# Packing the first query block's maxima scores into the PSUM banks of the third: ten pieces per group in place of eleven

## What is computed

```python
scores = jnp.einsum('bhsd,bhtd->bhst', xq, keys) * scale
scores = jnp.where(causal, scores, -jnp.inf)
probs = jax.nn.softmax(scores, axis=-1)
out = jnp.einsum('bhst,bhtd->bhsd', probs, values)
```

## Time and profile before

| what | value |
|---|---|
| median of 3 runs | 722.67 us |
| lowest and highest | 719.99 and 726.54 us |
| the profiled execution's own time | 722.22 us |
| its span, first to last instruction | 720.5 us (1.7 us lie outside it) |
| PE busy | 687.2 us, 95% of the span |
| DVE, ACT, POOL busy | 413.9, 293.0, 237.1 us |
| attention stage | about 70 to 345 us of the span |

### The profile page before, as it was taken

The page is one execution under the profiler, slowest core; times in us unless marked ns, Lnnn a source line. Parts: engine busy times, 40 slices in busy tenths (PEclk is TensorE's granted clock), DMA queues, the critical chain, the costliest instruction groups (busy, mean ns, idle before and its releaser), DMA issues. The chain is left out here.

```text
span 720.5 us, 10111 instructions
## 1 busy us (share of the span) xinstructions
PE 687.2 (95%) x3606; PEld 518.6 (72%) x3606; DVE 413.9 (57%) x982; ACT 293.0 (41%) x548; POOL 237.1 (33%) x241
## 2 busy tenths in 40 slices
PE   8998999999999999999999999789999999978998
PEld 6876666666666666666787788567888888766886
DVE  6735966766767676663477630485455544634611
ACT  4213345555545555454345132363434344322321
POOL 4465022322322232222245344232234222203443
PEclk9999999999999999999999999879999999997999
DMA  9328615123213333111356300210001100103211
GB/s 293 111 89 236 130 45 148 46 73 73 73 42 92 86 82 73 49 41 46 105 154 200 136 1 1 56 53 29 30 30 48 41 30 1 41 2 101 60 58 59
DMA packets 23146, 55.19 MB, mean 77 GB/s; under 512 B 3732, under 2 KB 4088, under 8 KB 22040
## 3 DMA queue, kind: packets, MB, share of 16 engines
q1 hardware_dynamic: 22840, 54.41, 26.5%
q10 hardware_dynamic: 256, 0.13, 0.1%
HBM read 42.86 MB, written 11.54 MB: 75 GB/s over the span
## 5 line engine op out<-in xcount | busy, mean ns | idle before, releaser
L964 DVE CUSTOM_DVE_ANT_0 bank<-bank,mask 128x512 f32<-128x512 f32 (+3 forms) x256 | 118.3, 521 | 60.8 <-PE bank L1018 60.5
L219 POOL TENSOR_TENSOR up_w_lo<-up_w_eff,up_w_hi 128x512 fp32r<-128x512 f32 x50 | 66.3, 1335 | 121.2 <-ACT up_w_hi L215 121.2
L372 POOL TENSOR_TENSOR down_h_lo<-hidden,down_h_hi 128x512 fp32r<-128x512 f32 x50 | 65.8, 1316 | 106.7 <-ACT down_h_hi L367 106.6
L52 PE MATMUL bank<-x0T_hi,up_w_hi 128*128 128x512 f32 x224 | 96.5, 431 | 3.8 <-POOL up_w_lo L219 2.3
L918 ACT ACTIVATE probs<-bank 128x512 f32<-128x512 f32 x160 | 85.1, 597 | 28.1 <-PE bank L1040 25.4
L54 PE MATMUL bank<-x0T_lo,up_w_hi 128*128 128x512 f32 x224 | 89.0, 398 | 0.0
L53 PE MATMUL bank<-x0T_hi,up_w_lo 128*128 128x512 f32 x224 | 89.0, 397 | 0.0
L52 PE MATMUL bank<-down_w_hi,down_h_hi 128*128 128x512 f32 x200 | 79.4, 397 | 1.1 <-DVE down_w_lo L357 0.7
L883 POOL TENSOR_SCALAR_AFFINE_SELECT probs<-probs 128x512 f32<-128x512 f32 x64 | 40.0, 638 | 120.8 <-ACT probs L918 120.8
L53 PE MATMUL bank<-down_w_hi,down_h_lo 128*128 128x512 f32 x200 | 78.9, 395 | 0.0
L54 PE MATMUL bank<-down_w_lo,down_h_hi 128*128 128x512 f32 x200 | 78.9, 395 | 0.0
(11 more groups left out here) (146 smaller groups left out, 1271.8 us busy)
## 6 DMA issues: line engine op xcount, KB each, us to landing
w_raw<-in_w_gate_up SPq DMA_DIRECT2D x25, 512.0 KB, 4.1
w_raw<-in_w_down SPq DMA_DIRECT2D x25, 256.0 KB, 2.8
q_stack<-q_hi SPq DMA_DIRECT2D x32, 128.0 KB, 3.4
att<-att_T SPq DMA_DIRECT2D x16, 256.0 KB, 2.0
q_hi<-rope_hi SPq DMA_DIRECT2D x8, 256.0 KB
q_lo<-rope_lo SPq DMA_DIRECT2D x8, 256.0 KB
q_stack<-q_lo SPq DMA_DIRECT2D x16, 128.0 KB, 3.7
attention_or_xn<-att SPq DMA_DIRECT2D x16, 128.0 KB
```

The source lines that it names most:

```text
L52: pe.matmul(out, w_hi, m_hi, start=first, stop=False, skip_group_check=True)
L219: pool.tensor_tensor(self.half(self.w_lo[:, o % 2], k), self.half(self.w_eff, k), f32(self.half(self.w_hi[:, o % 2], k)), ALU.subtract).th ...
L372: pool.tensor_tensor(self.h_lo[:, k % 2, :], self.hid[:, o, b * S:(b + 1) * S], f32(self.h_hi[:, k % 2, :]), ALU.subtract).then_inc(self.h ...
L964: dve.tensor_tensor_reduce(out=own, in0=own, in1=e.mask[:, S - w:S], scale=1.0, scalar=NEG, op0=ALU.add, op1=ALU.max, accum_out=rmax[:, i, ...
```

## The change

Block 0 loses its own piece. Its four parts of 128 columns are put behind the four 384-column parts of block 2, in the same banks (384 + 128 = 512 columns). There are ten pieces per group, and the bursts take 2, 3, 3 and 2. Matmuls and reductions are the same 16 per group with the same shapes. On DVE, in burst k = 2 (pieces 5, 6, 7) only the first part of each piece is reduced ahead of the high negate, which now asks for 9 reductions (`MAX_HIGH`); the three second parts come behind it. Piece 4, in burst 1, has both its parts reduced there. Banks come free at other counts (`MAX_END`).

```diff
-MAX_PIECES = [(3, h, 1) for h in range(4)] + [(2, h, 1) for h in range(4)] + [(1, 0, 2), (1, 2, 2), (0, 0, 4)]
-MAX_END = [1, 2, 3, 4, 5, 6, 7, 8, 10, 12, 16]
-MAX_BURST = [(0, 2), (2, 5), (5, 8), (8, 11)]
+MAX_PIECES = [[(3, h)] for h in range(4)] + [[(2, h), (0, h)] for h in range(4)] + [[(1, 0), (1, 1)], [(1, 2), (1, 3)]]
+MAX_END = [1, 2, 3, 4, 6, 10, 11, 12, 14, 16]
+MAX_HIGH = 9
+MAX_BURST = [(0, 2), (2, 5), (5, 8), (8, 10)]
...
-            def maxima(g, p):
-                i, h, nh = MAX_PIECES[p]
-                dve.wait_ge(s1_mm, 11 * g + p + 1)
+            def maxima(g, p, parts):
+                dve.wait_ge(s1_mm, len(MAX_PIECES) * g + p + 1)
...
-                dve.wait_ge(reduced, NJ * REP * g + (8 if half else 16))
+                dve.wait_ge(reduced, NJ * REP * g + (MAX_HIGH if half else NJ * REP))
...
+                        late = s["at"] == 2
                         for p in range(*MAX_BURST[s["at"]]):
-                            maxima(s["maxima"], p)
+                            maxima(s["maxima"], p, range(1 if late else len(MAX_PIECES[p])))
                         if s["at"] >= 2:
                             negate(s["maxima"], 3 - s["at"])
+                        if late:
+                            for p in range(*MAX_BURST[s["at"]]):
+                                maxima(s["maxima"], p, (1,))
...
-                w = (i + 1) * P
-                bank = wide.bank(("maxima", g, p))
-                for n in range(nh):
-                    last = pe.matmul(bank[:, n * w:(n + 1) * w], qst[K, slot, h + n, i * P:(i + 1) * P], kst[K, slot, 0:w],
-                                     start=(n == 0), stop=(n == nh - 1), skip_group_check=True)
+                bank, at = wide.bank(("maxima", g, p)), 0
+                for i, h in MAX_PIECES[p]:
+                    w = (i + 1) * P
+                    last = pe.matmul(bank[:, at:at + w], qst[K, slot, h, i * P:(i + 1) * P], kst[K, slot, 0:w],
+                                     start=(at == 0), stop=((i, h) == MAX_PIECES[p][-1]), skip_group_check=True)
+                    at += w
                 last.then_inc(s1_mm, 1)
```

More of the change, by code:

```diff
@@ L954, in vector @@
         def vector(dve):
-            def maxima(g, p):
-                i, h, nh = MAX_PIECES[p]
-                dve.wait_ge(s1_mm, 11 * g + p + 1)
+            def maxima(g, p, parts):
+                dve.wait_ge(s1_mm, len(MAX_PIECES) * g + p + 1)
                 if p == 0 and g >= 1:
                     dve.wait_ge(neg_done, 2 * g)
-                w = (i + 1) * P
-                for n in range(nh):
-                    own = wide.bank(("maxima", g, p))[:, n * w:(n + 1) * w]
+                for n in parts:
+                    i, h = MAX_PIECES[p][n]
+                    w, at = (i + 1) * P, sum((m + 1) * P for m, _ in MAX_PIECES[p][:n])
+                    own = wide.bank(("maxima", g, p))[:, at:at + w]
                     dve.tensor_tensor_reduce(out=own, in0=own,
                                              in1=e.mask[:, S - w:S], scale=1.0, scalar=NEG, op0=ALU.add, op1=ALU.max,
-                                             accum_out=rmax[:, i, h + n:h + n + 1]).then_inc(reduced, 1)
+                                             accum_out=rmax[:, i, h:h + 1]).then_inc(reduced, 1)
             def negate(g, half):
-                dve.wait_ge(reduced, NJ * REP * g + (8 if half else 16))
+                dve.wait_ge(reduced, NJ * REP * g + (MAX_HIGH if half else NJ * REP))
                 if g >= 1:
```

## The result

The changed kernel takes 724.65 us, the median of 20 runs (723.83 to 726.96), against 722.67 us for the kernel before on the same chip (20 runs, 719.99 to 726.61). The ratio is 1.0029, with an interval of 1.0017 to 1.0041. The change costs some 2 us (2.0 between the medians, 2.1 by the ratio). The forecast was 0.5 us less; the time is inside its range and within the 1% that it called "same", but the sign is wrong and the measurement is good enough to say so.

The account below looks back on a forecast made before the run. PE, busy for 95% of the span, was taken to bound the kernel. -3.2 + 1.3 + 0.4 + 1.0 = -0.5 us on the profiled 722.22 gave 721.7 (722.2 on the median of 722.67), range 718.0 to 726.0.

Parts of the forecast that it names:

- Burst 3: PE, bursts with k = 3: without the four small matmuls each becomes 0.36 us shorter, at most 0.41.
- Masks hold the values: Values behind burst 3 wait for POOL's last mask, so 3.2 us is saved of 5.4 freed.
- The rival that they do not hold them: Values behind burst 3: all 15 groups give 0.36 us, sum -2.7, 720.0 us; chance 0.20.
- Burst 1: PE, bursts with k = 1: the added 128-column matmul fits inside the present time; nothing lost.
- Burst 2: PE, bursts with k = 2: alternating 384 and 128 columns cost 0.04 us each, 0.4 us lost in all.
- The lane rival: Maxima lane of burst 2: packed parts do not fit beside the keys, 0.19 us per burst, 724.7 us; chance 0.12.
- The far price: Maxima lane of burst 2: weight loads not overlapped, some 0.6 us per burst, 730.8 us; chance 0.02.
- The sign that was named for this term: PE, bursts with k = 2 take 0.94 us at most where the DMA is in time.
- The factor ahead of burst 3: F4.1, F7.1, F10.1 and F13.1 wait for piece 5's second part on DVE; 1.3 us lost.
- the step's own 0.51: Ahead of burst 31: negate starts at 192.64, factor at about 193.15, its bank freed by piece 5's second part.
- Group 0: Four 128-column reductions on DVE stand ahead of the gate that holds PE; 1.0 us lost.
- The clock, a rival with 0.06: Group 0: PE stands still some 1.5 us ahead of 84.67, half clock for 3.3 us costs 1.6, 723.8 us; chance 0.06.

Follow-up runs that it names:

- the late issue on ACT: The changed kernel with ACT's DMA issue for the high rows moved behind the two exponentials of burst 3: 722.31 us, ratio 0.9983.
- the factors' wait removed alone: The changed kernel with the second part of piece 5 reduced ahead of the high negate: 723.21 us, ratio 1.0001.
- the two edits together: The changed kernel with piece 5's second part ahead of the high negate and the high rows' DMA issue behind the exponentials: 720.30 us, ratio 0.9962.
- added products: The changed kernel with four unused products of 512 columns ahead of steps 8 and 16 in group 0: 724.32 us, ratio 1.0016.

## Why the prediction was wrong, point by point

- **Burst 3**: right. 0.39 us per burst (forecast 0.36, at most 0.41).
- **Masks hold the values**: right. 8 groups pass some 0.27 on, 4 nothing, 3 all; 2.5 us came back where 2.2 was forecast. The rival that they do not hold them is out: the late issue on ACT gave those 2.3 us back.
- **Burst 1**: right, nothing.
- **Burst 2**: the term of 0.04 was too small. 0.10 us in the bursts that no DMA holds, inside the bounds of 0 and 0.19, so 1.5 us and not 0.4. The lane rival (0.19, and +2.0 in all) was half true. The far price of 0.6 us per burst is out. The sign that was named for this term (0.94 us at most where the DMA is in time) spoke against it: 1.00.
- **The factor ahead of burst 3**: this step failed. "The second part can start 0.09 behind the negate" took a delay from other places; here POOL's mask holds the negate, and the part starts 0.38 behind it. 2.65 us, where the sum had 1.3. With the negate as a reduction the step's own 0.51 comes out as 0.48. The prediction also held that nothing of it is hidden by the wait for the masks; 0.12 to 0.17 us of each is, and the factors' wait removed alone gives 1.4 us.
- **Group 0**: the gate was right (1.0 forecast, 0.95 measured). The clock, a rival with 0.06, was put at nothing in the sum. It was held unlikely for a gap of 1.19 us at full clock, and one such gap at full clock was weak evidence. In six of the eight profiles with new pieces in group 0 the clock fell between 84.3 and 86.4, about where the rival put it, for 1.5 us in five of them; the rival's price was 1.6. The changed kernel's own profile is not one of the six: there it fell at 74.0, ahead of all that the change moved, and the 1.4 us that this cost are chance.

Together: the forecast's -0.5, +1.3 for burst 2 with its DMA waits (1.7 in place of 0.4), +1.35 for the factors, +0.3 for the values, +1.4 for the clock and -0.5 for the larger saving in burst 3 (5.9 in place of 5.4) make +3.35 us, against 3.3 between the two profiled executions. Without the clock it is +1.95, so the factors and burst 2 alone turn the sign. The medians differ by 2.0. That this equals the sum without the clock does not show that the clock costs nothing as a rule, for the fall behind the gate stood in most profiles of this kind. DMA waits and the half clock's place and length differ from execution to execution; how much of the 2.0 us is due to either stays open. The step that failed is the factor's: 2.65 us where the sum had 1.3.

## What to carry to other kernels

Time taken out of one lane of a stage is worth what the next wait leaves of it. Follow the chain behind it (here transpose, copy, DMA issue, exponential, mask) and shorten that with it: the two edits together gave more than each of them alone. Before a length from a row is used as an instruction's cost, compare it with the same instruction elsewhere, and where it is longer look which other engine's instruction ends with it.

## What was not expected of the hardware

- Beside a mask on POOL a negate of 128x8 elements on DVE lasts 0.16 us as a reduction and 0.46 us, in places up to 0.62, as a multiplication, ending with the mask.
- A column of 384 and one of 128 do not pace like 512: 0.28 us against 0.23, in the same half of the rows.
- A DMA issue in ACT's queue takes 0.58 us there, and an exponential behind it waits for it; that is as long as an exponential of 512 columns.
- A stop of PE of 1.25 to 1.58 us, for the gate or in one variant for a bank, where the kernel before stops for 0.34, went ahead of a clock granted at 0.50, for 3.4 to 6.9 us, in six of eight profiles of the new group 0; in none of five with the old one. A fall at 74 us came in three of the thirteen profiles, with old pieces and with new ones. The one profile with added products in these places stays at 1.00.
